# One signal per pair of steps from TensorE, and one wait per pair of gathers on GpSimd

## The chip, the cores and the metric

The kernel runs on one core of a Trainium2 chip. The metric is the device time of one execution in microseconds (us). An execution at the profiler is a run of its own, with its own time; its span is the time from the first to the last recorded instruction.

## The reference

The reference is one layer of a graph network over 6250 nodes of 256 features and 200,000 edges. Everything is float32. With `xn = layernorm(x)`:

- the graph part: `weight[r] = sum_b w_comp[r, b] * bases[b]`, a message `xn[src] @ weight[edge_type] * edge_weight` for each edge, the sum of the messages at each edge's `dst`, and relu. There are 32 edge types and 8 bases;
- the mixing part: a linear attention with 8 heads over all nodes of `xn`, a layer norm, a two-layer network over `[xn, message]`, and another layer norm;
- `x + graph + mixing` is then normed again and goes through 8 experts of three 256 x 256 layers each, weighted by one softmax over the experts for each row.

This case is about the graph part. The edges are sorted by `dst`, and the sum over edges is formed as a chain of matrix products.

## The kernel before

**Steps.** A step takes 128 edges that lie in one chunk of 128 and whose `dst` lies in one group of 16 nodes. GpSimd gathers the 128 rows `xn[src]` from the DRAM tensor `normed_nodes` into one of 16 places of `ring` (RING = 16), 256 numbers for each partition. VectorE makes the step's selection matrix of 128 x 128: entry (edge, node n, basis b) is the edge's coefficient for basis b if its `dst` is node n of the group, else 0. TensorE multiplies: two products of 128 x 128 (one for each half of the features), which the chip executes as four MATMUL instructions for a step, into one of four places in PSUM (`slot(k)`, line 321). VectorE adds the result to the running sum of the group (`acc`, line 1306), where `keepc` is 1 if the step before belonged to the same group, else 0. SyncE stores four sums at a time to the DRAM tensor `step_sums`. Later the sums of 8 groups at a time are loaded back and multiplied with the bases.

**Iterations and blocks.** UN = 16 steps are one iteration; there are 123 iterations, 1968 steps. The first 24 are written out; the other 99 are 11 turns of a loop of 9 iterations (a block of 144 steps), which starts at about 1037 us. A loop needs register instructions that work out the number a wait compares with; the written-out part has constants. Between the steps the order written out by hand in `block_its` (one such function for each engine: lines 596, 1605 and 1951) places the mixing part of some tiles of 128 rows and the experts' layers for an earlier block.

**The counters.** Each engine runs its own list of instructions and meets the others at semaphores. Those that matter here:

- `mm_done`: TensorE adds 1 after each step (line 1738), and RING = 16 once at the start (line 1726), since all 16 places of the ring are free then.
- `row_in0` to `row_in7`: one for each pair of places of the ring; each gather adds 16. TensorE waits for both gathers of a pair before the pair's first step (line 1733).
- `acc_done`: VectorE adds 1 for each sum (line 1308). TensorE waits, once a pair, until the places in PSUM are free (line 1734).
- `sel_ready`: VectorE adds 1 for each four selection matrices (line 1273).
- `passed`: a helper, `wait_apart` (lines 325 to 329), waits and then adds 1 to this counter. Nobody waits for `passed`.

**Who reads `mm_done`.** GpSimd's `steps` (lines 742 to 748) waits before each gather until the step that used the same place one iteration earlier is done. VectorE's `pair` (line 1299) waits until both steps of a pair are done before it adds them. VectorE's `select` (line 1268) waits until the steps that used the same half of the selection buffer are done; its callers in `ahead` (lines 1310 to 1329) pass counts that are multiples of four steps.

GpSimd has nothing else to do in the stretch of the steps: its list is the wait for the next 16 indices (`idx_ready`, line 743, written by VectorE at line 1276) and then 16 times wait and gather. The gathers are DMAs whose descriptors GpSimd writes itself.

Of the kernel before, what the change touches and what calls it, by code (L numbers as in the profile page):

```python
# [42 lines left out]
UN = 16  # L43
BATCH = 4
NB = UN // BATCH
RING = UN
# [30 lines left out]
ALEAD = 3  # L77


def gps_layer(nc, x, src, dst, etype, eweight, bases, w_comp, Wq, Wk, Wv, Wm, W1, W2, g1, b1, g2, b2,  # L80
              Wr, br, fW1, fb1, fg1, fbe1, fm1, fv1, fW2, fb2, fg2, fbe2, fm2, fv2, Wo, bo, out):
    ctx = ExitStack()
    with ctx:
# [609 lines left out]
        @block.gpsimd  # L693
        def _(pool):
            dma_ahead(pool, "s_scat", len(LED_DMA))

            const = Chain(pool, "pool_const")

            def iota(o, pattern, cm=0):
                const(pool.iota(o, pattern, base=0, channel_multiplier=cm, allow_small_or_imprecise_dtypes=True))  # L700

            iota(iota16[:, :], [[1, GN]])
            iota(super_at[:, :], [[SGROUPS, SUPERS]])
            iota(group_no[:, :], [[P, 4]], 1)
            iota(super_no[:, :], [[1, SUPERS]])
            iota(chunk_no[:, :], [[P, CB]], 1)
            iota(slot_no[:, :], [[P, SB]], 1)
            for q in range(4):
                iota(relcol[32 * q:32 * q + 32, :], [[0, 1]], 1)
            pool.wait_ge(sem("dve_const"), 1)  # L710
            const(pool.affine_select(out=ident[:, :], in_=ident[:, :], compare_op=ALU.not_equal, fill=1.0, base=0,
                                     pattern=[[-1, P]], channel_multiplier=1))
            pool.wait_ge(sem("dve_const"), 8)

            const(pool.affine_select(out=rowmask[:, :], in_=rowmask[:, :], compare_op=ALU.is_gt, fill=0.0, base=NODES,
                                     pattern=[[-P, TILES]], channel_multiplier=-1))

            pool.wait_ge(sem("flag_ready"), 1)
            unsorted = pool.value_load(flag[0:1, 0:1], min_val=0, max_val=1)
            with pool.If(unsorted > 0):  # L720
                pool.iota(s_iota, [[1, SORTK]], base=0, channel_multiplier=0,
                          allow_small_or_imprecise_dtypes=True).then_inc(sem("s_const"), 1)
                pool.wait_ge(sem("s_fill"), 3)

                pool.affine_select(out=s_low, in_=s_low, compare_op=ALU.is_gt, fill=0.0, base=0,
                                   pattern=[[1, P]], channel_multiplier=-1).then_inc(sem("s_const"), 1)
                with pool.Fori(0, CHUNKS) as i:
                    wait_apart(pool, "s_recs", i + 1)
                    pool.indirect_dma_start(out=srt, out_offset=bass.IndirectOffsetOnAxis(ap=s_idx, axis=0),
                                            in_=s_rec, in_offset=None).then_inc(sem("s_scat"), 16)  # L730


            pool.wait_ge(sem("rec_ready"), 1)
            with pool.Fori(0, SB // 4) as i:
                for u in range(4):
                    wait_apart(pool, "col_ready", 8 * i + 2 * u + 2)
                    pool.indirect_dma_start(out=irec[:, u, :], out_offset=None, in_=rec,
                                            in_offset=bass.IndirectOffsetOnAxis(ap=colc[:, u:u + 1], axis=0)
                                            ).then_inc(sem(f"irec_in{u}"), 16)
            pool.wait_ge(sem("xn_ready"), 1)  # L740

            def steps(it, u):
                pool.wait_ge(sem("idx_ready"), it + 1)
                for k in range(UN):
                    wait_apart(pool, "mm_done", it * UN + k + 1)
                    pool.indirect_dma_start(out=ring[:, k, :], out_offset=None, in_=xnD,  # L746
                                            in_offset=bass.IndirectOffsetOnAxis(ap=idxc[:, u, k:k + 1], axis=0)
                                            ).then_inc(sem(f"row_in{k // 2}"), 16)

            with pool.Fori(0, ITERS // SETS) as i:  # L750
                for u in range(SETS):
                    steps(SETS * i + u, u)
# [250 lines left out]
        def _(dve):  # L1003
# [283 lines left out]
            coefs(0)  # L1287
            indices(0, 0)
            for q in range(2):
                select(0, q, RING)  # L1290
            dve.wait_ge(sem("grow_in"), 32)
            dve.wait_ge(sem("tables_ready"), 1)
            keeps(0)
# [2 lines left out]

            def pair(it, p):

                dve.wait_ge(sem("mm_done"), it * UN + 2 * p + 2 + RING)
                if p == 0:  # L1300
                    dve.wait_ge(sem("keepc_ready"), it + 1)
                for k in (2 * p, 2 * p + 1):
                    dve.wait_ge(sem("acc_done"), it * UN + k + ALEAD)
                    if k % BATCH == 0:
                        dve.wait_ge(sem(f"step_out{k // BATCH}"), DLEAD + 16 * it)
                    dve.scalar_tensor_tensor(acc[:, k % ACCR, :], acc[:, (k - 1) % ACCR, :], keepc[:, k:k + 1],  # L1306
                                             PS[:, slot(k):slot(k) + C], ALU.mult, ALU.add
                                             ).then_inc(sem("acc_done"), 1)

            def ahead(it, p, u):  # L1310

                s = it * UN
                if p == 0:
                    indices(it + 1, u + 1)
                if p == 1:
                    select(it, 2, s + BATCH + RING)
                if p == 2:
                    rel_hot(it + 1)
                if p == 3:
                    select(it, 3, s + 2 * BATCH + RING)  # L1320
                if p == 5:
                    coefs(it + 1)
                    dst_hot(it + 1)
                if p == 6:
                    select(it + 1, 0, s + 3 * BATCH + RING)
                if p == 7:
                    select(it + 1, 1, s + 4 * BATCH + RING)
                    dve.wait_ge(sem("acc_done"), s + UN + ALEAD)
                    keeps(it + 1)

            def m1_k(t):
# [56 lines left out]
            it = M1_ITS - 1  # L1388
# [283 lines left out]
        def _(pe):  # L1672
# [50 lines left out]
            pe.wait_ge(sem("table_cp"), LEAD + SB)  # L1723
            mm(bank(B_ACC, 0, KH * (P + 1)), zrow[:, 0:P], zrow[:, :])
            coef_mm(0)
            pe.sem_inc(sem("mm_done"), RING)

            def step(it, k):
                s = it * UN + k
                if k % BATCH == 0:  # L1730
                    pe.wait_ge(sem("sel_ready"), LEAD + NB * it + k // BATCH + 1)
                if k % 2 == 0:
                    pe.wait_ge(sem(f"row_in{k // 2}"), 32 * it + 32)
                    pe.wait_ge(sem("acc_done"), s - 2 + ALEAD)
                sel = selm[:, (k // BATCH) % 2, k % BATCH, :, :].rearrange("p n b -> p (n b)")
                for h in range(KH):
                    last = mm(PS[:, slot(k) + h * P:slot(k) + (h + 1) * P], ring[:, k, h * P:(h + 1) * P], sel)
                last.then_inc(sem("mm_done"), 1)

            def turn(o, frm, name):  # L1740

# [283 lines left out]
```

## Time and profile before

| | |
|---|---|
| three timed runs | 4190.02, 4193.39, 4204.43 us; median 4193.39 |
| profiled execution | 4209.15 us, span 4207.4 us |
| TensorE, matmuls / weight loads | 3357.9 us (80%) / 2955.5 us (70%) |
| VectorE | 2255.9 us (54%) |
| ScalarE | 800.3 us (19%) |
| GpSimd | 1949.4 us (46%), 2001 instructions |
| mean granted clock of TensorE | 0.920 |
| gathers, line 746 | 1968, 1931.2 us busy, mean 981 ns |
| sums, line 1306 | 1968, 944.7 us busy, mean 480 ns |
| matmuls of the steps | 7872, 1267.4 us busy |

How to read it: the busy times are of one profiled execution. PE is TensorE's matmul side and PEld its weight loads, which overlap it; DVE is VectorE, ACT ScalarE, POOL GpSimd, SP SyncE. A "q" behind an engine (DVEq) is its sequencer, which handles register and semaphore instructions; these are not counted as busy. Matmuls are pipelined, so the recorded durations overlap and a group of matmuls is shorter than their sum. All matmuls carry line 1674, a helper's, so they are told apart by the tiles they read: `PS<-steps` are the steps. `steps` is also the name of the large buffer that holds the ring, the sums and the selection matrices. "issue" as a releaser means that nothing visible ended the wait, and "remote" or "another core or an unknown queue" that the event was not recorded.

### The profile page before, as it was taken

Reading aid. Unit: us, or ns where it says so; the run is one execution under the profiler, and the core shown is the slowest. Engines: PE = TensorE matmul, PEld = TensorE weight load, DVE = VectorE, ACT = ScalarE, POOL = GpSimd, SP = SyncE. Lnnn points to the kernel's source line nnn. Section 1 sums busy time; section 2 is a strip of 40 time slices with the busy share of each in tenths; the row PEclk is TensorE's granted clock in tenths of the full one; section 3 lists DMA queues with packets and bytes.
Section 4 is the critical chain, followed back from the end, with each engine's and each line's share of the span. In section 5 each row is a group of like instructions: output and inputs, shape, how many; then the busy total and the mean of one; then the engine's idle time right before and its main releaser. Section 6 shows DMA issues by size and latency. Waiting matters only on the chain.

```text
span 4207.4 us, 68614 instructions
## 1 busy us (share of the span) xinstructions
PE 3357.9 (80%) x18778; PEld 2955.5 (70%) x18778; DVE 2255.9 (54%) x6008; ACT 800.3 (19%) x1546; POOL 1949.4 (46%) x2001
## 2 busy tenths in 40 slices
PE   0179976686988889898898888888888888888887
PEld 0157765575877868788787787877877778777675
DVE  5634465555555565555555555555555555555422
ACT  0023420001112121121211212112121221211233
POOL 0132246655555555555555555555454555555100
PEclk9999987887999999999899998998989999899899
DMA  6467776666766667676676766767667676676532
GB/s 195 128 194 237 241 206 189 198 194 207 235 206 219 211 219 239 201 230 208 210 232 208 229 210 209 228 217 226 204 210 231 214 219 216 208 237 207 163 103 80
DMA packets 647245, 864.29 MB, mean 205 GB/s; under 512 B 63829, under 2 KB 524195, under 8 KB 646686
## 3 DMA queue, kind: packets, MB, share of 16 engines
q1 hardware_dynamic: 510962, 549.74, 40.0%
q0 software_dynamic: 95776, 262.27, 21.8%
q10 hardware_dynamic: 40140, 47.81, 3.4%
q8 instruction: 179, 2.93, 0.3%
q14 instruction: 188, 1.54, 0.1%
HBM read 551.97 MB, written 316.84 MB: 206 GB/s over the span
## 4 chain that ended last, share of the span: by engine, by line
PE 53%; issue 11%; DVE 9%; another core or an unknown queue 5%; ACT 3%; DVEq 1%; SPq 0%; DMA 0%; ACTq 0%
PE PS L1674 53%; DVE steps L1306 4%; ACT feed L926 1%; DVE steps L1270 1%; DVE feed L1602 1%; ACT h_high L925 0%; ACT mixbuf L902 0%; DVE h_low L1005 0%; PE PS L1743 0%; ACT mixbuf L896 0%; DVE lst L1415 0%; DVE mixbuf L1437 0%; DVE lnr L1005 0%; DVE mixbuf L1005 0%
## 5 line engine op out<-in xcount | busy, mean ns | idle before, releaser
L746 POOL DMA_INDIRECT steps<-normed_nodes,steps x1968 | 1931.2, 981 | 1781.9 <-PE PS L1674 877.3
L1306 DVE SCALAR_TENSOR_TENSOR steps<-steps,PS 128x256 f32<-128x256 f32 x1968 | 944.7, 480 | 1599.5 <-PE PS L1674 1107.1
L1674 PE MATMUL PS<-steps 128*128 128x128 f32 x7872 | 1267.4, 299 | 316.6 <-issue 133.3
L1674 PEld LDWEIGHTS PS<-steps 128*128 128x128 f32 x7872 | 1169.1, 211 | 422.6 <-issue 257.7
L926 ACT ACTIVATE feed<-PS,bnc 128x512 f32<-128x512 f32 x416 | 319.9, 774 | 825.5 <-PE PS L1674 547.4
L1674 PE MATMUL PS<-bases_s,feed 128*128 128x256 f32 x1664 | 440.7, 408 | 0.0
L1674 PEld LDWEIGHTS PS<-bases_s,feed 128*128 128x128 f32 x1664 | 416.4, 334 | 6.2
L1270 DVE TENSOR_TENSOR steps<-steps 128x512 f32<-128x512 f32 x494 | 337.3, 683 | 0.1
L1674 PE MATMUL PS<-w_one,feed 128*128 128x256 f32 (+1 forms) x1028 | 309.5, 427 | 5.8 <-ACT feed L926 5.8
L925 ACT ACTIVATE h_high<-PS,bnc 128x512 fp32r<-128x512 f32 x208 | 161.6, 777 | 794.5 <-PE PS L1674 724.4
L1674 PE MATMUL PS<-h_high,split_in 128*128 128x512 f32 x832 | 276.0, 458 | 16.8 <-ACT feed L926 16.7
L1674 PE MATMUL PS<-x1t_high,split_in 128*128 128x512 f32 x832 | 261.6, 439 | 2.7 <-DMA w_one<-in_L_ffn_Wo_dram 2.3
L1602 DVE SCALAR_TENSOR_TENSOR feed<-PS,rw,feed 128x256 f32<-128x256 f32 x416 | 181.6, 479 | 111.7 <-PE PS L1674 106.1
L1674 PE MATMUL PS<-w_zero,feed 128*128 128x256 f32 x832 | 226.6, 402 | 6.7 <-ACT feed L926 6.7
L1674 PEld LDWEIGHTS PS<-w_one,feed 128*128 128x128 f32 x1028 | 179.5, 193 | 46.0 <-issue 24.7
L1674 PEld LDWEIGHTS PS<-h_high,split_in 128*128 128x128 f32 x832 | 163.8, 217 | 47.2 <-ACT feed L926 21.3
L1674 PE MATMUL PS<-w_s,mixbuf 128*128 128x256 f32 x416 | 122.7, 446 | 87.5 <-ACT mixbuf L902 50.0
L1674 PEld LDWEIGHTS PS<-wblk,steps 128*128 128x128 f32 x992 | 141.1, 217 | 65.5 <-DVE feed L1524 34.9
L1674 PE MATMUL PS<-wblk,steps 128*128 128x32 f32 x992 | 143.6, 292 | 49.7 <-DVE feed L1524 30.2
L1674 PEld LDWEIGHTS PS<-x1t_high,split_in 128*128 128x128 f32 x832 | 153.2, 202 | 27.0 <-DMA w_one<-in_L_ffn_Wo_dram 2.7
L1674 PEld LDWEIGHTS PS<-w_zero,feed 128*128 128x128 f32 x832 | 154.0, 204 | 25.5 <-ACT feed L926 11.3
L1005 DVE TENSOR_TENSOR h_low<-feed,h_high 128x1024 fp32r<-128x1024 f32 x104 | 127.3, 1224 | 69.1 <-ACT feed L926 63.5
(208 smaller groups left out, 2881.3 us busy)
## 6 DMA issues: line engine op xcount, KB each, us to landing
step_sums<-steps SPq DMA_DIRECT2D x492, 512.0 KB
split_in<-expert_split SPq DMA_DIRECT2D x104, 1024.0 KB
feed<-step_sums SPq DMA_DIRECT2D x416, 128.0 KB
steps<-step_types SPq DMA_DIRECT2D x125, 256.0 KB
steps<-normed_nodes,steps POOLq DMA_INDIRECT x1968
mixbuf<-mix_hidden SPq DMA_DIRECT2D x53, 256.0 KB
w_zero<-in_L_ffn_Wo_dram SPq DMA_DIRECT2D x52, 256.0 KB
w_one<-in_L_ffn_Wo_dram SPq DMA_DIRECT2D x52, 256.0 KB
```

Of the source, the lines that this page charges most:

```text
L746: pool.indirect_dma_start(out=ring[:, k, :], out_offset=None, in_=xnD, in_offset=bass.IndirectOffsetOnAxis(ap=idxc[:, u, k:k + 1], axis=0) ...
L925: act.activation(h1_high[:, k, :], bank(b0 + k), ACT.Relu, bias=bias, scale=scale)
L926: act.activation(o[:, k, :], bank(b0 + k), ACT.Relu, bias=bias, scale=scale).then_inc(sem(f"f_h{s}"), 1)
L1005: return dve.tensor_tensor(o, a, b, op)
L1270: dve.tensor_tensor(selm[:, q % 2, :, :, :], hot[:, s, :].unsqueeze(3).to_broadcast([P, BATCH, GN, BASES]), coef[:, s, :].unsqueeze(2).to_ ...
L1306: dve.scalar_tensor_tensor(acc[:, k % ACCR, :], acc[:, (k - 1) % ACCR, :], keepc[:, k:k + 1], PS[:, slot(k):slot(k) + C], ALU.mult, ALU.ad ...
L1602: dve.scalar_tensor_tensor(oacc[:, j, :], o_part(j), rw[:, EXPERTS * j + e:EXPERTS * j + e + 1], oacc[:, j, :], ALU.mult, ALU.add).then_in ...
L1674: return pe.matmul(o, a, b, start=start, stop=stop)
```

## The change

TensorE adds 1 to `mm_done` only after the second step of a pair, and RING / 2 = 8 at the start. All counts that others compare with are halved accordingly: 8 for an iteration instead of 16. GpSimd waits before the first gather of a pair until both of its places are free, and issues the second gather without a wait of its own. The wait for `acc_done` at the end of `ahead` keeps its count, now written out with `it * UN`.

```diff
@@ steps, on GpSimd
                 for k in range(UN):
-                    wait_apart(pool, "mm_done", it * UN + k + 1)
+                    if k % 2 == 0:
+                        wait_apart(pool, "mm_done", it * (UN // 2) + k // 2 + 1)
                     pool.indirect_dma_start(out=ring[:, k, :], out_offset=None, in_=xnD,
@@ on VectorE, before the first iteration
             for q in range(2):
-                select(0, q, RING)
+                select(0, q, RING // 2)
@@ pair
-                dve.wait_ge(sem("mm_done"), it * UN + 2 * p + 2 + RING)
+                dve.wait_ge(sem("mm_done"), it * (UN // 2) + p + 1 + RING // 2)
@@ ahead
-                s = it * UN
+                s = it * (UN // 2) + RING // 2
...
-                    select(it, 2, s + BATCH + RING)
+                    select(it, 2, s + BATCH // 2)
...
-                    select(it, 3, s + 2 * BATCH + RING)
+                    select(it, 3, s + BATCH)
...
-                    select(it + 1, 0, s + 3 * BATCH + RING)
+                    select(it + 1, 0, s + 3 * BATCH // 2)
                 if p == 7:
-                    select(it + 1, 1, s + 4 * BATCH + RING)
-                    dve.wait_ge(sem("acc_done"), s + UN + ALEAD)
+                    select(it + 1, 1, s + 2 * BATCH)
+                    dve.wait_ge(sem("acc_done"), it * UN + UN + ALEAD)
                     keeps(it + 1)
@@ on TensorE
-            pe.sem_inc(sem("mm_done"), RING)
+            pe.sem_inc(sem("mm_done"), RING // 2)
@@ step
-                last.then_inc(sem("mm_done"), 1)
+                if k % 2:
+                    last.then_inc(sem("mm_done"), 1)
```

## Rows read from the trace of the kernel before

**Rows 1.** The page: busy time and instructions of each engine.

```profile
PE 3357.9 (80%) x18778; PEld 2955.5 (70%) x18778; DVE 2255.9 (54%) x6008; ACT 800.3 (19%) x1546; POOL 1949.4 (46%) x2001
```

**Rows 2.** The page: the chain that ended last, by engine and line.

```profile
PE 53%; issue 11%; DVE 9%; another core or an unknown queue 5%; ACT 3%; DVEq 1%; SPq 0%; DMA 0%; ACTq 0%
PE PS L1674 53%; DVE steps L1306 4%; ACT feed L926 1%; DVE steps L1270 1%; DVE feed L1602 1%; ACT h_high L925 0%; ACT mixbuf L902 0%; DVE h_low L1005 0%; PE PS L1743 0%; ACT mixbuf L896 0%; DVE lst L1415 0%; DVE mixbuf L1437 0%; DVE lnr L10
```

**Rows 3.** View of the gathered tile: the gathers, who waited for them.

```profile
L746 POOL DMA_INDIRECT steps<-normed_nodes,steps x1968: 940/946/1991, 226.8 to 3924.3; - x197
...
  PE PS L1674: 6.9, 1
```

**Rows 4.** Who waited for whom: us in total, times, longest us.

```profile
DVE steps L1306 <- PE PS L1674: 1107.1, 486, 6.6
POOL steps L746 <- PE PS L1674: 877.3, 521, 6.8
...
POOL steps L746 <- issue: 440.5, 1298, 3.6
...
POOL steps L746 <- DVE steps L1276: 371.6, 96, 14.7
...
PE PS L1674 <- DVE steps L1306: 130.1, 82, 11.4
```

**Rows 5.** Groups by line up to 722.8 us, timeline, groups up to 734.5.

```profile
L746 POOL DMA_INDIRECT steps<-normed_nodes,steps x206 | 197.8, 960 | 312.8 <-PE PS L1674 196.1 <-DVE steps L1276 69.3 <-issue 33.1
...
L1674 PE MATMUL PS<-steps 128*128 128x128 f32 x768 | 124.9, 304 | 46.4 <-DVE steps L1306 26.4 <-issue 14.2 <-DVE steps L1270 5.8
...
721.82 0.95 POOL L746 DMA_INDIRECT steps<-normed_nodes,steps  x1 [0.30 <-PE PS L1674]
...
L1674 PE MATMUL PS<-steps 128*128 128x128 f32 x820 | 133.5, 305 | 47.6 <-DVE steps L1306 26.4 <-issue 14.2 <-DVE steps L1270 7.0
```

**Rows 6.** Timeline, 226 to 234.5 us: second gather, TensorE's first step.

```profile
228.30 0.95 POOL L746 DMA_INDIRECT steps<-normed_nodes,steps  x1 [0.30 <-issue]
...
234.04 0.76 PE L1674 MATMUL PS<-steps 128*128 128x128 f32 x2 [3.58 <-issue]
```

**Rows 7.** Groups up to 2030.4 us; windows (PE PEld DVE ACT POOL, clock, DMA).

```profile
L746 POOL DMA_INDIRECT steps<-normed_nodes,steps x940 | 918.7, 977 | 899.4 <-PE PS L1674 460.6 <-issue 204.8 <-DVE steps L1276 177.0
...
L1674 PE MATMUL PS<-steps 128*128 128x128 f32 x3708 | 603.6, 304 | 176.7 <-DVE steps L1306 83.5 <-issue 60.5 <-DVE steps L1270 31.9
...
2107.00:2371.00 264.00, 228.46 (x1265) 203.99 (x1266) 149.37 (x391) 50.47 (x86) 142.35 (x145) 0.92 0.69 218
```

**Rows 8.** Timeline of TensorE: steps alone, in twos and threes.

```profile
3482.68 1.05 PE L1674 MATMUL PS<-steps 128*128 128x128 f32 x8
...
3485.75 0.61 PE L1674 MATMUL PS<-steps 128*128 128x128 f32 x4
...
3501.13 1.50 PE L1674 MATMUL PS<-steps 128*128 128x128 f32 x12
```

**Rows 9.** View of the tile of steps: duration ns min/median/max.

```profile
L1674 PE MATMUL PS<-steps x7872: 269/275/583, 234.0 to 3951.5; 128*128 128x128 f32 x197
```

**Rows 10.** GpSimd's waits (L329) and register instructions (L328), ns min/median/max.

```profile
L329 POOLq EVENT_SEMAPHORE  x1984: 17/17/17, 183.2 to 3923.6; - x199
...
L328 POOLq ALU_OP  x1857: 32/32/49, 183.9 to 3919.7; - x186
```

**Rows 11.** Timeline of GpSimd: gathers with nothing to wait for.

```profile
2044.43 0.94 POOL L746 DMA_INDIRECT steps<-normed_nodes,steps  x1 [0.30 <-issue]
...
2048.29 0.95 POOL L746 DMA_INDIRECT steps<-normed_nodes,steps  x1 [0.30 <-issue]
```

**Rows 12.** VectorE's register instructions by line, ns min/median/max.

```profile
L1299 DVEq ALU_OP  x781: 40/40/45, 1043.0 to 3951.1; - x196
...
L1303 DVEq ALU_OP  x1386: 40/40/40, 1040.7 to 3951.8; - x198
...
L1666 DVEq FUSED_REGOPS  x11: 85/85/92, 1036.7 to 3691.3; - x11
```

## The prediction

> **What bounds the kernel now.** I read the engines' busy shares first, then the chain of work that ended last, then who waited for whom, and last the stretches in which the changed signal is produced and used.
>
> TensorE is the busiest engine, 80% of the span as matmul and 70% as weight load; VectorE has 54% and GpSimd 46% [rows 1]. The chain says the same: 53% of it is TensorE, 9% VectorE, 11% "issue" (time with no visible releaser), 5% unknown, and the gather of GpSimd, line 746, is not among the lines it lists [rows 2]. So the reader should look for what the change gives to TensorE or VectorE, or to the hand-over between them; GpSimd's own time counts only if TensorE runs out of gathered rows.
>
> It does not. In the view of the gathered tile, TensorE waited for a gather once, 7 us, at the very start [rows 3]. The other direction is long: GpSimd waited 877.3 us in 521 places for TensorE and 371.6 us for VectorE's list of indices, while 1298 of the 1968 gathers had only a short gap before them [rows 4]. GpSimd is the engine that follows; it refills a place a whole turn of the ring, 16 steps, before it is read.
>
> How far ahead is it where the lead is shortest? Up to 722.8 us it had started 206 gathers, the last at 721.82, and TensorE had done the matmuls of 768 / 4 = 192 steps; up to 734.5 us TensorE had issued 820 matmuls, so it began its 206th step just after [rows 5]. The 206th gather thus started about 12.7 us before its use. A gather needs less: at the start, with no lead at all, the second one began at 228.30 and TensorE used it at 234.04, 5.7 us later [rows 6]. The margin at that narrow place is 12.7 - 5.7 = 7.0 us. In the loop of blocks it is wider: up to 2030.4 us, 940 gathers and 3708 / 4 = 927 steps, 13 steps of lead; one step takes about 264 / 144 = 1.8 us there [rows 7], so some 24 us.
>
> **The change, part by part.** The sum is made against the profiled execution, 4209.15 us with a span of 4207.4; the median of the three timed runs is 4193.39, 15.8 us or 0.4% lower, and the forecast is that median plus the sum.
>
> 1. *TensorE: 984 increments fewer* (one per pair of 1968 steps). The increment rides on a matmul; what could be saved is a delay behind it. A step alone, four matmuls, takes 0.61 us; two steps in a row, eight matmuls with one increment between, take 1.05; three in a row 1.50 [rows 8]. With 0.275 us for the last matmul (the median in [rows 9]) the spacing inside a step is (0.61 - 0.275) / 3 = 0.112 us. The next four matmuls add 0.44 to 0.45, that is 4 x 0.111. The increment's own share is 0.445 - 4 x 0.112 = 0.00, by rounding between -0.02 and +0.02. I take 0. Bounds: 984 x 0.02 = 20 us of TensorE's time either way, of which 53% lies on the chain, 10 us.
>
>  A rule of the Trainium skill speaks for a gain here: TensorE: Matmul & The Clock Gate, The cost: per-tile semaphore tail, has increments of matmuls serialize at 26.3 ns each. By it the sum would hold up to 984 x 0.0263 = 26 us less, an estimate from that page. By that rule the spacing behind a step would be wider than inside one; this trace shows no such difference.
>
> 2. *GpSimd: 984 waits fewer, with their count of passed waits and one register instruction each.* Recorded are 1984 of these waits at 17 ns and 1857 register instructions at 32 ns [rows 10], so 984 x 0.049 = 48 us of its queue. Between two gathers with nothing to wait for lie 0.30 us [rows 11]; the second gather of a pair may start up to 0.30 us sooner, at least 0. That is at most 984 x 0.30 = 295 us of GpSimd's time, all of it in an engine that the end does not wait for [rows 2, 3]. Worth 0; if the cover were gone it would be a gain.
>
> 3. *GpSimd: the first gather of a pair waits for the second step.* This is the added wait. Behind it on the queue stand both gathers and the next wait for indices. Where GpSimd is waiting for TensorE, the first gather starts later by the distance of two steps, and the second starts 1.25 us behind the first (0.95 + 0.30, [rows 11]) where before it could start with its own signal. So the pair is complete at most 1.25 us later, and the first row up to 6.8 us later, the longest wait of GpSimd [rows 4]. TensorE waits for both rows of a pair together before and after, so only the completion counts: 1.25 against a margin of 7.0 at the narrow place. Worth 0. What is late next is nothing: GpSimd is behind anyway by the time VectorE's indices come. Ends: 0, and the rival below.
>
> 4. *VectorE: the same waits, other numbers.* pair() waited for the even count of steps, so it is released by the same matmul as before. What can differ is how the numbers are made: in the loop each is a register instruction of 40 ns, 781 of them for line 1299, and 1386 for the counter of finished sums, line 1303, which is 14 for each of 99 iterations where 16 waits stand [rows 12]. So two of 16 values are shared with another wait's. With mm_done counted by 8 an iteration and acc_done by 16 that sharing may go: 2 x 99 x 40 ns = 8 us. The nearest row for a form with a multiplication is the 85 ns of line 1666, once per block [rows 12], so I bound a dearer form by 792 x (85 - 40) ns = 36 us. Value: one dearer instruction per iteration, 99 x 45 ns = 4 us, plus 8 us is 12 us in VectorE's queue; the chain has 10% in VectorE and its queue, so 1 us. Ends: -1 and 44 us.
>
> 5. *DMA: the gathers move by 0.3 us earlier to some 2 us later.* The 16 DMA engines are 69% busy in the block loop [rows 7], with as many bytes as before. A shifted gather can push a store or a load of the VectorE path either way. No row prices it; I take 0 and give it a share of both outer cases.
>
> Sum: 0 + 0 + 0 + 1 + 0, rounded to no change: **4193 us**.
>
> **Rivals.**
>
> *A. Increments do cost TensorE* (faster). For it: GpSimd and VectorE both listen to this counter, and 11% of the chain is unexplained issue time [rows 2]. Against it: the equal spacing in [rows 8]. With 0.02 us each, 984 x 0.02 = 20 us on an engine that is nearly always the bound: 4173 us. The same place holds the page's 26 us, 4167 by that estimate.
>
> *B. VectorE's numbers get dearer* (slower). Place: the register instructions at lines 1299, 1303 and 1268, which stand directly before the sums that TensorE waits for (130.1 us of TensorE's waits name line 1306, [rows 4]). Price: 8 + 36 = 44 us if every wait in the loop pays the full difference and none is hidden; half of it, 22 us, gives 4215 us. It decides from the point at which VectorE arrives at the wait after the signal; against it stand 1107.1 us in which VectorE was there first and waited for TensorE [rows 4], where a dearer number is hidden.
>
> *C. The paired wait starves TensorE* (slower). From the point at which a pair completes later than its margin, 7.0 us at the narrowest, TensorE would wait. In the 24 iterations before 1047 us one such place each at 1.25 us gives 30 us, 4223. Against it: 1.25 is far under 7.0.
>
> *D. The moved transfers help or hurt* by chance: TensorE's path meets them through stores and loads only. Some 15 us to either side, 4178 or 4208.
>
> *E. The change does not do what it says on GpSimd*: the 0.30 us between gathers may be the gather's own start and not the wait's, and stay. The time is then 4193 all the same; it changes only what the trace shows.
>
> **How the numbers follow.** A measurement of this kernel tells about 0.3%, 12.6 us, from no change (the three runs span 14.4 us). No change, with E inside it: 0.68, range 4181 to 4206. A: 0.11. D faster: 0.07. D slower: 0.05, partly within the bound. B: 0.07. C: 0.02. So faster 0.18, same 0.68, slower 0.14. The range takes in A's 4173 and nearly all of B's 4215: 4172 to 4214.
>
> **What would show it.** In the changed trace: GpSimd still has 1968 gathers, but its waits halve; gaps between the two gathers of a pair are 0.30 or less, never a wait for TensorE; TensorE still waits for a gather only at the start; groups of four, eight and twelve step matmuls keep 0.61, 1.05 and 1.50 us. Wrong if the group of eight shrinks by 0.02 or more (A), if line 1299 shows dearer or line 1303 more instructions and VectorE's waits shrink while TensorE's grow (B), or if TensorE waits for the gathered tile in the loop (C). A shift in waits on transfers, with none of these, is D.

## The result, and the profile after

| | before | after |
|---|---|---|
| timed side by side, five runs each | 4196.30 us median (4190.02 to 4210.12) | 4166.18 us median (4156.79 to 4171.74) |
| ratio | 1 | 0.9917, interval 0.9892 to 0.9942 |
| profiled execution | 4209.15 us, span 4207.4 | 4166.18 us, span 4164.4 |
| mean granted clock of TensorE, profiled execution | 0.920 | 0.909 (the other four runs 0.910 to 0.925) |

The change made the kernel 0.8% faster by the ratio, 30 us (0.7%) between the medians; a second comparison further down gave 0.9881. I had forecast no change.

The page of the changed kernel, busy time and instructions of each engine, and the chain by engine and line:

```profile
PE 3348.7 (80%) x18778; PEld 2958.6 (71%) x18778; DVE 2256.7 (54%) x6008; ACT 799.8 (19%) x1546; POOL 1951.1 (47%) x2001
```

```profile
PE 50%; issue 9%; DVE 8%; another core or an unknown queue 4%; ACT 3%; DVEq 1%; SPq 0%; DMA 0%; ACTq 0%
```

No engine has less to do, beside [rows 1]. TensorE's busy time fell by 9.2 us, its idle time from 4207.4 - 3357.9 = 849.5 to 4164.4 - 3348.7 = 815.7 us, that is by 33.8. So almost four fifths of the 43.0 us between the two spans is TensorE standing still less. The chain names the same engines and causes, none of those listed with a larger share [rows 2].

Who waited for whom in the changed kernel (us in total, times, longest us):

```profile
DVE steps L1307 <- PE PS L1675: 1118.8, 465, 6.9
POOL steps L747 <- PE PS L1675: 846.6, 369, 5.5
...
POOL steps L747 <- issue: 469.3, 1445, 2.1
...
DVE steps L1307 <- remote: 332.5, 108, 16.3
POOL steps L747 <- DVE steps L1277: 326.8, 102, 14.7
...
PE PS L1675 <- issue: 162.6, 152, 6.5
PE PS L1675 <- DVE steps L1307: 139.8, 102, 11.5
```

Two rows of the same view of the kernel before that the prediction did not use:

```profile
DVE steps L1306 <- remote: 326.2, 82, 17.7
...
PE PS L1674 <- issue: 204.9, 143, 6.9
```

Beside [rows 4] three things moved. GpSimd's waits for TensorE are fewer (521 to 369 places), as the edit says. Its wait for VectorE's list of indices is 45 us shorter (371.6 to 326.8). And TensorE's waits without a visible releaser fell from 204.9 to 162.6 us, 42 us, nearly the whole difference of the spans. But that row is not steady: in a second trace of the same changed kernel (the last of the fourth group below) it is 183.5 us. TensorE's wait for the sums rose by 10 us. The gathered tile still held TensorE up once, at the start (6.1 us, before 6.9, [rows 3]).

The groups of step matmuls in the timeline of the changed kernel, one, two and three steps long, are what they were in [rows 8]:

```profile
3437.64 1.50 PE L1675 MATMUL PS<-steps 128*128 128x128 f32 x12
...
3449.80 1.05 PE L1675 MATMUL PS<-steps 128*128 128x128 f32 x8
...
3451.55 0.61 PE L1675 MATMUL PS<-steps 128*128 128x128 f32 x4
```

A gather of GpSimd in the changed kernel with nothing to wait for; GpSimd's waits and their register instructions; and VectorE's at the line of the pair's wait and at the counter of sums (ns min/median/max):

```profile
2041.87 0.94 POOL L747 DMA_INDIRECT steps<-normed_nodes,steps  x1 [0.30 <-issue]
```

```profile
L329 POOLq EVENT_SEMAPHORE  x1000: 17/17/17, 183.2 to 3889.5; - x167
```

```profile
L328 POOLq ALU_OP  x873: 32/32/49, 183.8 to 3886.1; - x175
...
L328 POOLq FUSED_REGOPS  x123: 37/37/53, 225.9 to 3867.7; - x123
```

```profile
L1300 DVEq ALU_OP  x693: 40/40/45, 1034.9 to 3916.5; - x174
L1300 DVEq FUSED_REGOPS  x88: 53/53/53, 1059.3 to 3890.8; - x88
```

```profile
L1304 DVEq ALU_OP  x1474: 40/40/45, 1032.8 to 3917.3; - x185
```

The gap before a gather that waits for nothing is still 0.30 us. Passed waits went from 1984 to 1000 [rows 10], as the edit says. VectorE has 88 instructions at 53 ns where there were 40 ns, and 88 more at line 1304 [rows 12]: 88 x 13 + 88 x 40 ns = 4.7 us.

The gain is not in one place. Measured from a turn's first step to the next turn's, the turns of 144 steps took 265.3 us in the mean before and 262.9 after, so 24 us over the ten turns that can be measured so. Before the loop it was 8 us ahead, and up to about 640 us nothing was gained.

### The profile page after: what moved, and what is told of

Its sections match the earlier page's. It is cut to its first block, busy times and chain, and to the rows that moved or that the text cites. A ratio compares the mean times of both kernels' runs of the same rounds, so it can differ in the third digit from the quotient of the medians.

```text
span 4164.4 us, 66745 instructions
## 1 busy us (share of the span) xinstructions
PE 3348.7 (80%) x18778; PEld 2958.6 (71%) x18778; DVE 2256.7 (54%) x6008; ACT 799.8 (19%) x1546; POOL 1951.1 (47%) x2001
## 4 chain that ended last, share of the span: by engine, by line
PE 50%; issue 9%; DVE 8%; another core or an unknown queue 4%; ACT 3%; DVEq 1%; SPq 0%; DMA 0%; ACTq 0%
PE PS L1675 50%; DVE steps L1307 3%; ACT feed L927 1%; DVE steps L1271 1%; DVE feed L1603 1%; ACT h_high L926 0%; PE PS L1745 0%; DVE h_low L1006 0%; DVE lst L1416 0%; DVE mixbuf L1438 0%; ACT mixbuf L897 0%; ACT mixbuf L903 0%; DVE steps L1252 0%; DVEq L1304 0%
## 5 line engine op out<-in xcount | busy, mean ns | idle before, releaser
L747 POOL DMA_INDIRECT steps<-normed_nodes,steps x1968 | 1932.9, 982 | 1747.5 <-PE PS L1675 846.6
L1675 PEld LDWEIGHTS PS<-wblk,steps 128*128 128x128 f32 x992 | 131.8, 203 | 59.0 <-DVE feed L1525 35.8
L1675 PE MATMUL PS<-mixbuf,w1b_s 128*128 128x128 f32 x832 | 136.4, 316 | 43.1 <-ACT mixbuf L897 28.2
L1675 PE MATMUL PS<-wblk,steps 128*128 128x32 f32 x992 | 132.1, 279 | 46.8 <-DVE feed L1525 33.1
```

Of the source, the lines that this page charges most:

```text
L1675: return pe.matmul(o, a, b, start=start, stop=stop)
```

## The experiments

Each kernel was run beside the kernel before on the same chip, and one of its executions was profiled. "Ratio" is always to the kernel before on that chip. An edit is shown against the kernel before where nothing else is said. Each of the five groups below ran on a chip of its own; the kernel before took 4216.50 us (median) in the first, 4272.33 in the second, 4216.16 in the third, 4212.22 in the fourth and 3743.96 in the fifth. A sum called "remote" is the sum of all rows of the waits view whose releaser is "remote"; it is 807 us in the kernel before and 787 in the changed one (839 in its second trace). In the stretch that is shown further down, "remote" is not an event that was not recorded: the signal that ended the wait is in the trace, but no instruction that raises it had ended just before.

### First group: which part of the change is it?

**One part alone: TensorE signals once per pair, GpSimd keeps a wait before each gather.**

```diff
# against the changed kernel
-                    if k % 2 == 0:
-                        wait_apart(pool, "mm_done", it * (UN // 2) + k // 2 + 1)
+                    wait_apart(pool, "mm_done", it * (UN // 2) + k // 2 + 1)
```

> The changed kernel, but GpSimd waits before both gathers of a pair (both waits compare with the same count, so the second is always met). TensorE has the 984 increments fewer. Theory 1 (TensorE's increments cost): all of the gain stays, ratio to the kernel before about 0.992. Theory 2 (the waits of GpSimd cost): the gain is gone, 0.998 to 1.002. Theory 3 (the gathers start at other times, and other transfers with them): the gain stays nearly whole, 0.991 to 0.995, since the gathers start later as in the changed kernel.

Measured: 4184.40 us, ratio 0.9916 (0.9886 to 0.9946).

**The other part alone: TensorE signals each step, GpSimd waits once per pair.**

```diff
-                    wait_apart(pool, "mm_done", it * UN + k + 1)
+                    if k % 2 == 0:
+                        wait_apart(pool, "mm_done", it * UN + k + 2)
```

> The kernel before, but GpSimd waits once per pair, for the second step. TensorE signals each step. Theory 1 (increments): no gain, 0.998 to 1.002. Theory 2 (GpSimd's waits): the whole gain, about 0.992. Theory 3 (other start times of the gathers): the whole gain, about 0.992.

Measured: 4155.48 us, 0.9847 (0.9811 to 0.9882).

**The changed kernel with its missing increments given to a counter that nobody reads.**

```diff
# against the changed kernel
-                if k % 2:
-                    last.then_inc(sem("mm_done"), 1)
+                last.then_inc(sem("mm_done" if k % 2 else "spare"), 1)
```

> The changed kernel, but the last matmul of each even step increments a semaphore that nobody waits for, so TensorE has as many increments as before. Theory 1: the gain is gone, 0.998 to 1.002. Theories 2 and 3: the gain stays, about 0.992.

Measured: 4155.81 us, 0.9855 (0.9819 to 0.9891).

**The kernel before with twice the increments.**

```diff
                 for h in range(KH):
                     last = mm(PS[:, slot(k) + h * P:slot(k) + (h + 1) * P], ring[:, k, h * P:(h + 1) * P], sel)
-                last.then_inc(sem("mm_done"), 1)
+                    last.then_inc(sem("mm_done" if h else "spare"), 1)
```

> The kernel before, but the first half's matmul of each step also increments a semaphore that nobody waits for: 1968 increments more. Theory 1: slower by twice the gain of the change, 1.016. Theories 2 and 3: no change, 0.998 to 1.002.

Measured: 4215.40 us, 1.0006 (0.9983 to 1.003).

What follows: the increments cost nothing that these runs can measure. All of them back leaves the gain whole, and 1968 more add nothing. Nor are VectorE's other numbers the cause: the kernel with only GpSimd's line changed has VectorE as before and gains as much. Both halves of the change "alone" give the gain, and what these two have in common is that the first gather of a pair waits for the second step. The first of the four gained less than the second and third, by 0.6 to 0.7% on one chip. It is also the only one of the three with the second wait of each pair still there, so this could be a small price of the waits; the next group bounds it, and does not explain it.

### Second group: fewer waits, or later gathers?

**Two waits as before, but both for the pair's second step.**

```diff
-                    wait_apart(pool, "mm_done", it * UN + k + 1)
+                    wait_apart(pool, "mm_done", it * UN + (k | 1) + 1)
```

> The kernel before, with a signal for each step and a wait for each gather, but the first gather of a pair waits for the second step too: only its start is later. Theory 3 (the later start brings the gain, whatever the number of waits): 0.985 to 0.992, like the changed kernel. Theory 2 (the number of GpSimd's waits brings it): 0.998 to 1.002.

Measured: 4229.01 us, 0.9906 (0.9886 to 0.9925).

**The kernel before with the wait of line 745 written twice.**

> The kernel before with a second wait, always met, before each gather: 1968 waits more in GpSimd's list, no gather later. Theory 2: slower by up to twice the gain, 1.010 to 1.016. Theory 3: 0.998 to 1.002.

Measured: 4282.99 us, 1.0014 (0.9995 to 1.0032).

**One wait for four gathers** (`if k % 4 == 0:` and a count of `k + 4`).

> The kernel before with one wait before each four gathers, for all four steps. Theory 2: half as many waits go again, ratio 0.975 to 0.980. Theory 3: three of four gathers start later by up to three steps, so the gain grows too unless TensorE begins to wait for gathers: 0.975 to 0.985. If two gathers back to back are the optimum: 0.985 to 1.000.

Measured: 4236.93 us, 0.9923 (0.9903 to 0.9943): no more than with one wait for two, and outside what every theory expected but the last.

**Each gather waits two steps longer than it must** (`k + 3` for `k + 1`).

> The kernel before, but each gather waits for the step two after its own: all gathers are later by two steps, none is bunched, and no wait is taken away. Theory 3 in its plain form (later is better): 0.980 to 0.992. If it is not the delay but that two gathers follow each other without a stop: 0.998 to 1.002. Theory 2: 0.998 to 1.002.

Measured: 4141.14 us, 0.9701 (0.9679 to 0.9723).

What follows: 1968 waits more cost at most 0.3%, and the later start alone, with every wait kept, gives 0.9906, the gain of the change (0.9917 and 0.9881) within the intervals. With all starts two steps later than in the kernel before it is 3%. The step of the change that I had priced at 0 is the one that works. GpSimd's wait for the indices shrank along with it (371.6 us before, 310.5 with both waits late, 58.3 with two steps more), but it is not the measure of the gain: with one wait for four gathers it is 40.0 us, and the gain is 0.8%.

### Third group: is later itself what helps?

The expectations of this group name a theory 4: long runs of gathers back to back hold up TensorE's signals.

**The gathers four steps later than they must be** (`k + 5`).

> The kernel before, each gather waiting for the step four after its own. Theory 4: still fewer long runs, since GpSimd is held to TensorE's pace: 0.955 to 0.970, unless TensorE begins to wait for gathers (lead 13 - 2 steps). Theory 3: the same. If two steps were the optimum: 0.970 to 0.985.

Measured: 4075.68 us, 0.9667 (0.9637 to 0.9697).

**Six steps later** (`k + 7`).

> The kernel before, each gather waiting for the step six after its own. Theories 3 and 4 if the lead still suffices: at or under the time with four, 0.950 to 0.970. If the lead is too short: over it, 0.97 to 1.00, with waits of TensorE for the gathered tile in the trace.

Measured: 4066.16 us, 0.9645 (0.9619 to 0.9672). The gain levels off, and TensorE begins to wait for gathered rows a little (11.2 us in 4 places of the step matmuls).

**The opposite cure: gathers as early as before, but VectorE writes the list of indices one iteration earlier**, so that GpSimd is not held for it.

```diff
@@ before the first iteration
             indices(0, 0)
+            indices(1, 1)
@@ ahead
-                    indices(it + 1, u + 1)
+                    indices(it + 2, u + 2)
```

> The kernel before, but VectorE writes the indices of an iteration one iteration earlier, so GpSimd no longer waits for them (371.6 us before) and its gathers start earlier, not later; also it has less to catch up on. Theory 4 (long runs of gathers back to back hold up TensorE's signals): fewer long runs, 0.975 to 0.995. Theory 3 (a later start is what helps): 1.000 to 1.010.

Measured: 4080.04 us, 0.9679 (0.9645 to 0.9713), as much as the late gathers and more than theory 4 expected. A gather starts 26.0 us before its step's first matmul in the mean, 25.7 in the kernel before, so none of this is a later start. Waits of this kernel:

```profile
PE PS L1675 <- issue: 169.2, 140, 3.9
...
DVE steps L1307 <- remote: 146.8, 62, 6.1
...
POOL steps L746 <- DVE steps L1276: 14.4, 1, 14.4
```

The wait for indices is gone (96 places before, 1 here). "Later is better" therefore falls as the cause of the 3%. What both cures share is fewer very long runs of gathers: runs of eight or more with under 0.6 us between them held 414 gathers in the kernel before, 149 with starts two steps later and 170 here. Shorter runs remain. The kernel before shows what happens in a long one. Its timeline from 2043 us, with other rows left out (start us, length us, engine, line; in brackets the idle time before it and the releaser):

```profile
2043.18 0.94 POOL L746 DMA_INDIRECT steps<-normed_nodes,steps  x1 [3.98 <-DVE steps L1276]
...
2044.89 1.06 PE L1674 MATMUL PS<-steps 128*128 128x128 f32 x8
...
2046.01 0.61 PE L1674 MATMUL PS<-steps 128*128 128x128 f32 x4
2046.14 0.49 DVE L1246 TENSOR_SCALAR steps<-steps,relcol 128x512 f32<-128x512 f32 x1 [0.20 <-DVE lnr L1005]
...
2047.32 0.61 PE L1674 MATMUL PS<-steps 128*128 128x128 f32 x4
...
2049.54 0.95 POOL L746 DMA_INDIRECT steps<-normed_nodes,steps  x1 [0.30 <-issue]
2050.41 1.00 DVE L1306 SCALAR_TENSOR_TENSOR steps<-steps,PS 128x256 f32<-128x256 f32 x2 [3.78 <-remote]
2050.79 0.95 POOL L746 DMA_INDIRECT steps<-normed_nodes,steps  x1 [0.30 <-issue]
...
2051.46 1.22 PE L1674 MATMUL PS<-steps 128*128 128x128 f32 x4 [2.67 <-issue]
...
2052.05 1.18 POOL L746 DMA_INDIRECT steps<-normed_nodes,steps  x1 [0.30 <-issue]
...
2054.89 0.99 DVE L1306 SCALAR_TENSOR_TENSOR steps<-steps,PS 128x256 f32<-128x256 f32 x2 [2.49 <-remote]
...
2055.38 0.94 POOL L746 DMA_INDIRECT steps<-normed_nodes,steps  x1 [2.16 <-remote]
```

GpSimd gets its list at 2043.18 after a wait of 3.98 us and issues eight gathers back to back, 0.30 us apart. TensorE does four steps early in it (eight, four and four matmuls); the first two are done by 2045.95, the fourth by 2047.93. VectorE has nothing to do from 2046.63 on and waits for nothing but the signal of the first two, yet its sums start at 2050.41, 4.5 us after their steps' end; the sums of the next two start at 2054.89, 7.0 us after. TensorE in turn stands for 2.67 us. After the run of gathers everything moves at once. The recorded signals of TensorE show it directly: one at 2047.43, one at 2050.30, then six of three counters between 2054.59 and 2054.88.

The whole trace agrees. Take for each recorded signal of TensorE how long after the end of the last matmul or weight load that raises its counter it came. (That is the least that it can have been late; some signals are missing in the record, and 23 of over 14 us, as many in every kernel within one, are left out.) Of 3181 signals 599 came over 1 us late; of VectorE's 4153 it is 2, of ScalarE's 1119 it is 1. Late signals go with runs of gathers: when the last gather was the first or second of its run and was still running or had ended less than 3 us before, 111 of 1533 were late (7%), when it was the third or fourth 59 of 423 (14%), when it was the fifth or a later one 427 of 829 (52%), and when the last gather had ended over 3 us before, 2 of 350.

So signals of TensorE arrive late while GpSimd issues gathers back to back. VectorE then falls behind; that this delays the next list of indices and so makes the next backlog is my reading; the gain of the early list fits it and does not isolate it.

**A pause before every pair of gathers.** GpSimd fills a small scratch tile that nobody reads and waits until that is done. The pace of the gathers falls; no other engine has another instruction.

```diff
+        pool_pad = sb("pool_pad", [P, 32])
...
                     wait_apart(pool, "mm_done", it * UN + k + 1)
+                    if k % 2 == 0:
+                        pool.memset(pool_pad[:, :], 0.0).then_inc(sem("pad"), 1)
+                        wait_apart(pool, "pad", it * (UN // 2) + k // 2 + 1)
```

> The kernel before with a short memset on GpSimd, and a wait for it, ahead of the first gather of each pair (it adds a scratch tile and computes nothing): the gathers may start as early as before, but a run of them has a gap after every second. Theory 4: 0.980 to 0.995, with TensorE's signals less late. Theory 3: the starts move by some tenths of a microsecond only, 0.998 to 1.003.

Measured: 3952.95 us, 0.938 (0.9354 to 0.9406). The timeline of GpSimd and the waits in this kernel:

```profile
2040.82 0.95 POOL L750 DMA_INDIRECT steps<-normed_nodes,steps  x1 [0.81 <-remote]
2042.08 0.95 POOL L750 DMA_INDIRECT steps<-normed_nodes,steps  x1 [0.30 <-issue]
2043.02 0.14 POOL L748 MEMSET pool_pad<- 128x32 f32 x1
2043.97 0.95 POOL L750 DMA_INDIRECT steps<-normed_nodes,steps  x1 [0.81 <-POOL pool_pad L748]
2045.23 0.95 POOL L750 DMA_INDIRECT steps<-normed_nodes,steps  x1 [0.30 <-issue]
```

```profile
PE PS L1678 <- DMA steps<-normed_nodes,steps: 133.6, 69, 5.4
```

```profile
PE PS L1678 <- issue: 90.6, 88, 5.4
```

```profile
DVE steps L1310 <- remote: 5.5, 1, 5.5
```

Two gathers now take 3.15 us at most pace (2040.82 to 2043.97) instead of 2.50, and the late signals are all but gone: 45 of 2691 came over 1 us late, 599 of 3181 before; "remote" is 10 us in all, 807 before, and TensorE's waits without a releaser fell from 204.9 to 90.6. TensorE even pays for it with 133.6 us of waiting for gathered rows, and the kernel is 6.2% faster all the same, far more than theory 4 had expected. Of the 251.4 us between the two profiled spans TensorE's busy time has 104.6 (3357.9 to 3253.3), and with it goes a higher mean granted clock (0.942, before 0.920); how much of the gain is the clock was not separated. This is the strongest evidence here that late signals cost time.

The same counts for the kernels of these groups (a long run is one of eight or more gathers with under 0.6 us between them):

| kernel | ratio | long runs (gathers in them) | signals of TensorE | over 1 us late | over 3 us late |
|---|---|---|---|---|---|
| before | 1 | 44 (414) | 3181 | 599 | 182 |
| changed | 0.9917 | 50 (446) | 2315 | 463 | 158 |
| both waits late | 0.9906 | 28 (252) | 3092 | 614 | 195 |
| one wait for four | 0.9923 | 90 (738) | 3029 | 594 | 244 |
| two steps later | 0.9701 | 16 (149) | 3046 | 652 | 103 |
| indices early | 0.9679 | 19 (170) | 3104 | 606 | 66 |
| four steps later | 0.9667 | 21 (189) | 3078 | 606 | 69 |
| six steps later | 0.9645 | 21 (185) | 3058 | 562 | 82 |
| pause for each pair | 0.938 | 0 | 2691 | 45 | 10 |
| pause for each fourth (below) | 0.9917 | 0 | 3148 | 592 | 213 |

The kernels that gain 3% have as many late signals as the kernel before, but far fewer very late ones (66 to 103 for 182), and the kernel that gains 6% has next to none. The kernels that gain 1% do not show it: the changed kernel has as many long runs as before and as large a share of late signals (20%, before 19%). What carries its gain is not in these counts.

### Fourth group: with the change, and what kind of pause

**The same pause in the changed kernel.**

> The changed kernel with the memset and the wait for it ahead of each pair, as in the run that spaced the kernel before (0.938). Theory 4, with the change's gain coming through the runs of gathers: once the runs are broken nothing is left for the change to gain, 0.934 to 0.942. If the change gains by something else as well: that much lower again, 0.928 to 0.932.

Measured: 3940.67 us, 0.9371 (0.9346 to 0.9396), faster than both kernels. The pause alone gave 0.938, so the change adds nothing on top. That fits a gain that comes through late signals, but does not prove it: GpSimd hardly ever has TensorE to wait for here (183 us in all, 846.6 in the changed kernel), so the change has few gathers left to start later.

**The pause before every fourth gather.**

> The kernel before with the memset and the wait ahead of every fourth gather, so that a run has at most four without a longer gap. Theory 4: signals were late from the fifth gather of a run on, so most of the gain is there with half the memsets, 0.938 to 0.955. If the gain comes from each memset or wait and not from the length of the runs: half of it, 0.965 to 0.975.

Measured: 4167.73 us, 0.9917 (0.9891 to 0.9944), a smaller gain than either theory expected. No run of gathers was longer than four here, and "remote" still sums to 594 us. Four gathers took 2.50 + 3.15 = 5.65 us, 1.41 each, against 1.58 with a pause for each pair and 1.25 without. So it is not the length of a run alone: 213 signals came over 3 us late with no run over four.

**The memset without waiting for it** (GpSimd waits for the memset of the pair before, which is long done).

> The kernel before with the same memset ahead of each pair, but GpSimd waits for the memset of the pair before, which is long done: the gap of 0.81 us shrinks to about 0.45. If any work between the gathers breaks the run: 0.938 to 0.950. If what counts is a gap in which GpSimd's queue stands empty: 0.985 to 1.002.

Measured: 4241.24 us, 1.0068 (1.004 to 1.0095), a little slower than either theory expected. GpSimd's timeline in it:

```profile
2042.30 0.95 POOL L751 DMA_INDIRECT steps<-normed_nodes,steps  x1 [0.17 <-POOL pool_pad L750]
2043.56 0.95 POOL L751 DMA_INDIRECT steps<-normed_nodes,steps  x1 [0.30 <-issue]
2044.51 0.14 POOL L750 MEMSET pool_pad<- 128x32 f32 x1
2044.81 0.95 POOL L751 DMA_INDIRECT steps<-normed_nodes,steps  x1 [0.17 <-issue]
```

The memset fits into the 0.30 us that lie between two gathers anyway, so the pace is that of before (2.51 us a pair) and "remote" sums to 925 us. The instruction itself does not help; the wait or the pause does.

**The changed kernel once more.**

> The changed kernel once more, beside the others on one chip: 0.985 to 0.993, by all theories.

Measured: 4160.53 us, 0.9881 (0.9853 to 0.9908); with the first comparison, 0.9917, the change is worth 0.8 to 1.2%.

### Fifth group: pace or emptied queue, on a chip that differs

**Four short memsets that nobody waits for.**

```diff
+            pool.sem_inc(sem("pad"), 1)
...
+                    if k % 2 == 0:
+                        wait_apart(pool, "pad", it * (UN // 2) + k // 2 + 1)
+                        for j in range(3):
+                            pool.memset(pool_pad[:, j * 8:(j + 1) * 8], 0.0)
+                        pool.memset(pool_pad[:, 24:], 0.0).then_inc(sem("pad"), 1)
```

> Kernel before, with four small GpSimd memsets of a scratch tile before each first gather of a pair; GpSimd waits only for the memsets of the pair before, which are long done, so its queue is never held for its own finish. The gap before a pair should be about as wide as in the version with one memset and a wait for it (0.8 to 0.9 us), without the emptied queue. Theory 'pace': what holds up TensorE's signals is the pace of the gathers; the ratio is then 0.93 to 0.95. Theory 'emptied queue': what helps is that GpSimd waits for its own last instruction to finish before it hands out further gathers; the ratio is then 0.99 to 1.01, as with the single memset that nobody waits for.

**The pause before every gather.**

> Kernel before, with a memset of a scratch tile and a wait for it before every gather, so that two gathers take about 3.5 us instead of 2.5 (before) or 3.0 (memset for each pair). Theory 'pace' and theory 'emptied queue' both expect at least the gain of the version with one for each pair: 0.93 to 0.945, unless GpSimd now runs out of lead: at 1.75 us per gather it is as slow as the steps (about 1.8 us each), TensorE would wait for the gathered tile, and the ratio would go to 0.95 or above.

Measured: 3769.98 us, ratio 1.0063 (1.0048 to 1.0079), and 4483.36 us, 1.1975 (1.1958 to 1.1992). But this chip ran the kernel before in 3743.96 us (3738.96 to 3752.56), 11% below the fastest median of any other chip here. GpSimd's timeline and TensorE's waits with the four memsets:

```profile
2757.18 0.95 POOL L753 DMA_INDIRECT steps<-normed_nodes,steps  x1 [0.15 <-POOL pool_pad L752]
2758.44 0.95 POOL L753 DMA_INDIRECT steps<-normed_nodes,steps  x1 [0.30 <-issue]
...
2759.77 0.95 POOL L753 DMA_INDIRECT steps<-normed_nodes,steps  x1 [0.15 <-POOL pool_pad L752]
```

```profile
PE PS L1681 <- issue: 8.6, 7, 2.9
```

The memsets gave 2.59 us a pair, not the 3.1 I wanted, so the kernel is no test of the pause. It shows something else: here GpSimd issues up to 48 gathers without a gap of 0.6 us, and not one wait has the releaser "remote"; 2 of TensorE's 3654 signals came over 1 us late, and its waits without a releaser are 8.6 us. On this chip runs of gathers do not hold the signals up. Whether the kernel before is as clean there was not traced; its time suggests that it is. A slower GpSimd then only costs: the pause before each gather makes it 0.95 + 0.95 = 1.90 us a gather, 1968 x 1.90 = 3739 us for GpSimd alone, and TensorE waits for gathered rows:

```profile
PE PS L1677 <- DMA steps<-normed_nodes,steps: 528.1, 242, 7.5
```

Neither the change nor the pause for each pair was timed on that chip.

## Why the prediction was wrong

1. *Increments, priced 0*: right. The spacing of [rows 8] is unchanged, and 1968 more increments cost 1.0006 (0.9983 to 1.003). Rival A, which named this gain, fell; so did the estimate of 26 us from the Trainium skill (TensorE: Matmul & The Clock Gate, The cost: per-tile semaphore tail). By the page's 26.3 ns, 1968 increments would be 52 us, or 1.2%, again an estimate from that page; the page states it for matmuls packed as tiles of the array, which these are not. The time fell where A put it, for another reason: that was luck.
2. *Fewer waits on GpSimd, priced 0*: right within 0.3%. Doubling them costs 1.0014 (0.9995 to 1.0032); the smaller gain of the kernel that kept its second wait (0.9916 beside 0.9847 and 0.9855) stays unexplained. The gap between gathers stayed 0.30 us with nothing to wait for, as rival E had it.
3. *The first gather of a pair waits for the second step, "Worth 0"*: **this is the step that failed.** Alone, with all waits kept, it gives 0.9906 (0.9886 to 0.9925), the whole change, where I had 0 or a loss. Its reasoning held as far as it went: TensorE waits for gathered rows no more than before, and rival C did not come. The error was the frame: I asked only whether the rows would be late, and so bounded the effect by 0 and a loss. That a gather started later could be a gain I never priced, although the rows for it were there: 371.6 us of GpSimd's waits for indices followed by gathers 0.30 us apart [rows 4, 11], and 11% "issue" and 5% unknown on the chain [rows 2], which I left unexplained in every other case than rival A.
4. *VectorE's numbers, priced 1 us, bounds -1 and 44*: right; 4.7 us of its queue after, and the kernel without them gains as well. Rival B fell.
5. *Moved transfers, "No row prices it; I take 0"*: the only place where the prediction let the start times matter, with 15 us to either side and 0.07 for faster. It gave both signs, so it named nothing. For the 3% and 6% kernels TensorE's signals are what the traces show; whether moved transfers have a part in the change's own 1% no run tests.

So the range's low end, 4172, came from a price for increments, and 4166 lay under it. The runs show in place of step 3: the later start is itself a gain, 1% with the first gather of each pair one step later, 3% with every gather two steps later. Behind the larger gains stands that on these chips TensorE's signals come late while GpSimd issues a run of gathers: very late ones are fewer in the 3% kernels, with later starts and with an earlier list of indices alike, and all but gone in the 6% one, with a pause for each pair.

How the change's own 1% comes about is not shown; that it is the later start is, by the edit in isolation. In its trace GpSimd waits less for indices and TensorE less for unseen releasers, but "remote" is nearly the same (787 and 839 in its two traces, 807 before), it has as many long runs as before, and 20% of its signals are late, 19% before. So nothing measured here accounts for it. The sum of "remote" does not rank the kernels either: it is 590 us with one wait for each pair and all signals (0.9847), 594 with the pause before each fourth gather (0.9917), and 640 with starts two steps later (0.9701).

**Still open:** by what way the change gains its 1%; what in back-to-back gathers holds the signals up, the pace or that GpSimd's queue never empties, since both memset versions without a wait kept the old pace; and why one chip does not show it.

## What to carry to other kernels

When an engine that nobody waits for follows behind the others, ask not only whether its work comes in time but in what bursts it issues it; a deliberate small pause, or a list prepared one iteration earlier, was worth 6% and 3% here, where the increments and the waits were worth nothing that could be measured. Waits with the releaser "remote" or "issue" on an engine whose operands were done microseconds before were late signals here: look what the other queues issue in such a stretch. A gain of this kind belongs to the chip as well as to the kernel, so time it on more than one before it is relied on.

## What the runs showed of the hardware

- TensorE's signals, steps done at 2045.95 and 2047.93 us, were acted on 4.5 and 7.0 us later while GpSimd issued eight indirect gathers of 128 rows at 1.25 us each. Over the whole trace 599 of its 3181 signals came over 1 us late, 52% of those that came after five or more gathers in a row and under 1% of those when no gather had ended in the last 3 us; of VectorE's 4153 signals 2 did. At 1.58 us a gather 45 of 2691 came late and the "remote" waits fell from 807 to 10 us; at 1.41 it was 592 of 3148 and 594 us.
- One program took 4196 to 4272 us (medians) in every other comparison and 3743.96 on one chip, where the traces of two variants show no such wait.
- A memset of 0.14 us on GpSimd between two gathers is free of time (2.51 us a pair, 2.50 without), and a memset with a wait for its end costs 0.65 us (3.15).
- An increment on a matmul costs nothing that these runs can measure: 1968 more gave 1.0006 (0.9983 to 1.003).
